# A four-layer graph network on one core: gathered edge rows for more target tiles and stages, tiles in another order

## The reference, cut to what matters

```python
h = relu(layernorm(x)); x = x + L0(h)   # hypergraph convolution, twice: m = segment_sum(xt[src], dst) / B
                                        #                                out = segment_sum(m[dst], src) / D
h = relu(layernorm(x)); x = x + L1(h)   # red = segment_sum(h[src] + relvectors[type], dst); GRU cell(red, h)
h = relu(layernorm(x)); x = x + L2(h)   # GCN: out = segment_sum(norm * (h @ W.T)[src], dst), self loops; layernorm; relu
h = relu(layernorm(x)); x = x + L3(h)   # attention: softmax over heads of the first n edges' two ends
```

## Time and profile before

| | us |
|---|---|
| three runs | 1287.16, 1292.99, 1293.87 (median 1292.99) |
| the profiled execution, its own time | 1292.79 |
| its span | 1289.8 |
| busy: PE, DVE, ACT, POOL | 1192.9 (92%), 701.2 (54%), 444.1 (34%), 269.8 (21%) |
| chain that ended last, by engine | PE 80%, DVE 7%, POOL 6%, DMA 2%, ACT 2%, issue 2% |

### The profile page before, as it was taken

One profiled execution on the slowest core, in us unless ns is written; L12 is line 12 of the kernel. 1 busy time (PEld: TensorE's weight loads), 2 busy tenths in 40 slices (PEclk: granted clock), 3 DMA queues, 4 the chain that ended last, 5 costly groups with the idle time before them and its releaser, 6 DMA issues.

```text
span 1289.8 us, 23482 instructions
## 1 busy us (share of the span) xinstructions
PE 1192.9 (92%) x9431; PEld 934.7 (72%) x9431; DVE 701.2 (54%) x1974; ACT 444.1 (34%) x948; POOL 269.8 (21%) x438
## 2 busy tenths in 40 slices
PE   2699999999999998989999999999999998999990
PEld 1456666768989995556888888676777767898970
DVE  7866456774555655545354552434435364655556
ACT  2745554428766651112112121221212222212123
POOL 6820000112000004566011110000100011355310
PEclk9989999999999999989999999999999999999995
DMA  4210000004122212322444331011101101122103
GB/s 169 73 32 1 1 2 1 1 1 162 64 69 77 76 64 81 104 77 83 127 145 167 133 113 59 25 38 32 43 25 38 37 30 55 34 59 61 36 9 101
DMA packets 48801, 80.77 MB, mean 63 GB/s; under 512 B 8617, under 2 KB 30597, under 8 KB 48688
## 3 DMA queue, kind: packets, MB, share of 16 engines
q1 hardware_dynamic: 37420, 54.52, 12.7%
q0 software_dynamic: 7136, 14.07, 3.9%
q10 hardware_dynamic: 4132, 10.63, 2.3%
HBM read 49.29 MB, written 29.89 MB: 61 GB/s over the span
## 4 chain that ended last, share of the span: by engine, by line
PE 80%; DVE 7%; POOL 6%; DMA 2%; issue 2%; ACT 2%; SPq 0%; DVEq 0%; ACTq 0%
PE ps L478 39%; PE ps L1992 11%; PE ps L817 5%; PE ps L2016 4%; PE ps L783 3%; PE ps L890 3%; PE ps L892 3%; PE ps L772 3%; PE ps L916 2%; POOL pairA L1699 2%; PE ps L896 2%; PE ps L894 2%; PE ps L862 1%; POOL whh L745 1%; POOL work L745 1%
## 5 line engine op out<-in xcount | busy, mean ns | idle before, releaser
L478 PE MATMUL ps<-big,pairB 125*128 125x250 fp8e4 (+1 forms) x2600 | 304.5, 268 | 0.6 <-DVE big L1255 0.6
L478 PEld LDWEIGHTS ps<-big,pairB 125*128 125x128 f16 x2600 | 239.6, 98 | 30.8 <-issue 2.8
L1992 PE MATMUL ps<-pairA,adj 125*125 125x512 f16 x625 | 208.1, 406 | 0.0
L727 POOL TENSOR_TENSOR st<-st,mhalf 125x1 f32<-125x1 f32 x100 | 62.0, 620 | 509.8 <-DVE st L1375 509.4
L478 PE MATMUL ps<-adj,pairB 125*128 125x250 fp8e4 (+1 forms) x1300 | 146.3, 267 | 1.8 <-DVE pairB L1433 1.8
L478 PE MATMUL ps<-adj,pairA 125*128 125x250 fp8e4 (+1 forms) x1300 | 139.2, 267 | 0.0
L478 PEld LDWEIGHTS ps<-adj,pairB 125*128 125x128 f16 x1300 | 123.3, 99 | 16.2 <-DVE pairB L1433 2.1
L478 PEld LDWEIGHTS ps<-adj,pairA 125*128 125x128 f16 x1300 | 120.9, 98 | 19.3 <-issue 7.7
L1929 ACT ACTIVATE adj<-ps 125x450 fp8e4<-125x450 f32 (+6 forms) x191 | 97.3, 518 | 103.5 <-PE ps L2018 103.0
L2018 PEld LDWEIGHTS ps<-wih 128*128 128x128 bf16 x615 | 84.6, 144 | 51.9 <-issue 1.3
L2018 PE MATMUL ps<-wih 128*128 128x7 bf16 (+5 forms) x615 | 101.9, 178 | 0.0
(11 more groups left out here) (316 smaller groups left out, 1841.8 us busy)
## 6 DMA issues: line engine op xcount, KB each, us to landing
t_adjTp<-big SPq DMA_DIRECT2D x25, 400.0 KB, 2.6
...
```

Of the source, the lines that this page charges most:

```text
L478: last = pe.matmul(out, src[:, j, FEAT * part + 128 * c:FEAT * part + 128 * (c + 1)], rhs(j, p), start=(n + part == 0 and not begun), stop ...
L727: g.tensor_tensor(st[:, 9:10], st[:, 8:9], k.mhalf[:, 0:1], ALU.pow).then_inc(S[rstd], 1)
L1992: last = pe.matmul(k.ps[0:P, 6 + t % 2, :], k.adj[:, j, PITCH * i:PITCH * i + P], k.pairA[:, j, :], start=(j == 0), stop=(j == TILES - 1))
```

## The change

1. Tiles 14 to 24 may be gathered. The lists of a tile are as many as its expected edges need (`LISTS`: 12, 11, 11, 11, 10, 10, 10, 10, 10, 9, 9 for tiles 14 to 24, 113 in all), not 10 for all.
2. In the build the first mean of tiles 17 to 24 (`BUILD_FAR`) is gathered: 79 lists instead of 8 x 25 dense matmuls. `ORDER` and the new `SUMS` (order of the means) differ, and `SUMMED` is spread evenly over the slots. The source rows are stored to `t_pairs` at the start of the build.
3. The second mean gathers tiles 18 to 24 as before (68 lists); its one-hots are all made in the first turns, in free columns of `adj`, and the ring has more buffers. `overlay` and `ballot` move to back1.
4. The GRU gathers tiles 14 to 24 (113 lists, four matmuls of 125 columns each), the GCN tiles 20 to 24 (48 lists, and four such matmuls for each tile's own row). Groups come in the order `GRU_GROUPS`, `GCN_GROUPS`. Each stage's input rows are stored to a table (two DMAs a tile) before its first gather.
5. POOL's list: gathers stand ahead of `deviation(i)` in the numbers of `GRU_PACE` and `GCN_PACE`; the z gathers stand behind by `BASE_PACE`.

By the tables 504 aggregate units stand in the build instead of 625 (`SUMMED` at slot 72: 35 instead of 75, at slot 136: 90 instead of 183), and 518 units in the second mean instead of 520.

```diff
-ORDER = tuple(range(TILES - 1, -1, -1))
+ORDER = (*range(16, 12, -1), *range(24, 19, -1), *range(12, 8, -1), 19, 18, *range(8, -1, -1), 17)
-SPARSE, EACH = 7, 10
-DENSE = TILES - SPARSE
-GATHERS = SPARSE * EACH
-AHEAD = 4
+FAR, BUILD_FAR, MEAN_FAR, GCN_FAR = 14, 17, 18, 20
+def list_length(tile):
+    share = math.sqrt((tile + 1) / TILES) - math.sqrt(tile / TILES)
+    mean = EDGES * share
+    return math.ceil((mean + 3.4 * math.sqrt(mean * (1 - share))) / SLOT)
+LISTS = [list_length(t) for t in range(FAR, TILES)]
+GATHERS = sum(LISTS)
+def list_of(tile):
+    at = sum(LISTS[:tile - FAR])
+    return range(at, at + LISTS[tile - FAR])
+FIRST_GATHER, GATHER_SLOTS = 168, 3.8
 def summing():
-    marks = [0, STOP[1] + 5] + [STOP[t] + 5 for t in range(2, TILES)]
-    share = [0, 0] + [TILES * (TILES - 1) * (t - 1) / (TILES - 2) for t in range(2, TILES)]
+    near, far = [i for i in ORDER if i < BUILD_FAR], list(range(TILES - 1, BUILD_FAR - 1, -1))
+    units = {i: TILES if i < BUILD_FAR else LISTS[i - FAR] for i in ORDER}
+    ready = {i: STOP[ORDER.index(i)] + 5 for i in near}
+    for n, i in enumerate(far):
+        ready[i] = max(STOP[ORDER.index(i)] + 30, FIRST_GATHER + 8 + GATHER_SLOTS * sum(units[t] for t in far[:n + 1]))
+    total, done, left, order, out = sum(units.values()), 0, 0, [], []
+    for s in range(SLOTS):
+        while done < total * (s - 32) / (SLOTS - 32):
+            if not left:
+                turn = next((x[0] for x in (far, near) if x and ready[x[0]] <= s and not (order and x is far and order[-1] >= BUILD_FAR)), None)
+                if turn is None:
+                    break
+                (far if turn >= BUILD_FAR else near).remove(turn)
+                order.append(turn)
+                left = units[turn]
+            left, done = left - 1, done + 1
+        out.append(done)
+    return order + near + far, units, out
-MEAN_GAPS = (4, 3, 2, 2, 3, 2, 2)
-MEAN_ORDER = [i for n, gap in enumerate(MEAN_GAPS)
-              for i in (*range(sum(MEAN_GAPS[:n]), sum(MEAN_GAPS[:n + 1])), DENSE + n)]
+MEAN_GAPS = (6, 2, 2, 2, 2, 2, 2)
+MEAN_ORDER = [i for n, gap in enumerate(MEAN_GAPS)
+              for i in (*range(sum(MEAN_GAPS[:n]), sum(MEAN_GAPS[:n + 1])), MEAN_FAR + n)]
+GRU_GROUPS = (0, 1, 2, 7, 3, 8, 4, 9, 5, 10, 6, 11, 12)
+GCN_GROUPS = (0, 1, 2, 3, 10, 4, 5, 11, 6, 7, 8, 9, 12)
+GRU_ORDER, GCN_ORDER = ([t for g in groups for t in range(2 * g, min(2 * g + 2, TILES))] for groups in (GRU_GROUPS, GCN_GROUPS))
+HOT_ORDER = [*range(MEAN_FAR, TILES), *range(FAR, MEAN_FAR)]
+def visiting():
     out = []
-    for s in range(SLOTS):
-        n = max(m for m, at in enumerate(marks) if at <= s)
-        part = (s - marks[n]) / (marks[n + 1] - marks[n]) if n + 1 < len(marks) else 0
-        upto = share[n] + part * (share[min(n + 1, TILES - 1)] - share[n])
-        out.append(min(TILES * sum(stop + 5 <= s for stop in STOP), round(upto)))
+    for stage, order, first in ((0, SUMS, BUILD_FAR), (1, MEAN_ORDER, MEAN_FAR), (2, GRU_ORDER, FAR), (3, GCN_ORDER, GCN_FAR)):
+        for turn, tile in enumerate(order):
+            if tile >= first:
+                start = out[-1].stop if out else 0
+                out.append(Visit(stage, tile, min(turn, 21) if stage == 3 else turn, start, start + LISTS[tile - FAR]))
+GRU_PACE = (22,) + (5,) * (TILES - 1)
+GCN_PACE = (14, 3, 3, 0, 0, 3, 3, 2, 2, 3, 3, 3, 0, 0, 0, 0, 0, 2, 3, 3, 1, 0, 0, 0, 0)
+BASE_PACE = (0, 0, 0, 3, 3, 0, 0, 1, 1, 0, 0, 0, 3, 3, 3, 3, 3, 2, 0, 0, 0, 0, 0, 0, 0)
...
+        def gather(q, n, s):
+            wait_past(pool, F["used"], max(HOME[n][1] + 1, VISITS[q - 3].stop if q >= 3 else 0))
+            g.indirect_dma_start(gathered(k, n), None, d["pairs2" if VISITS[q].stage == 3 else "pairs"], bass.IndirectOffsetOnAxis(ap=k.far_src[:, s:s + 1], axis=0)
+                                 ).then_inc(landed(k, q)[0], 16)
+        pool.wait_ge(k.paired, 2 * 32 * TILES)
+        for one in gathers(1):
+            gather(*one)
         for i in range(TILES):
             deviation(i, k.st[i % 2], B, "var", "rstd", "nmr")
+        pool.wait_ge(k.paired, 3 * 32 * TILES)
+        pool.wait_ge(indexed, 64)
+        waiting = gathers(2)
         for i in range(TILES):
-            deviation(i, k.st[i % 2], G, "var", "rstd", "nmr", k.dinvu)
+            for one in itertools.islice(waiting, GRU_PACE[i]):
+                gather(*one)
+            deviation(i, k.st[i % 2], G, "var", "rstd", "nmr", k.dinvu[:, GRU_ORDER[i]:GRU_ORDER[i] + 1])
+        pool.wait_ge(k.paired, 4 * 32 * TILES)
+        waiting = gathers(3)
         for i in range(TILES):
+            for one in itertools.islice(waiting, GCN_PACE[i]):
+                gather(*one)
             deviation(i, k.st[i % 2], C, "var", "rstd")
             deviation(i, k.st2[i % 2], C, "var2", "rstd2", "nmr2")
-            if i == 5:
+            if i == 3:
                 pool.wait_ge(T["hot"], 1)
                 pool.wait_ge(T["base"], 16)
-            if 5 <= i < 18:
-                for t in range(2 * (i - 5), min(2 * (i - 5) + 2, TILES)):
-                    g.indirect_dma_start(far_z(t), None, d["z0"][:, :], bass.IndirectOffsetOnAxis(ap=idx[:, 1, t:t + 1], axis=0)
-                                         ).then_inc(T["far"], 16)
+            for t in range(sum(BASE_PACE[:i]), sum(BASE_PACE[:i + 1])):
+                g.indirect_dma_start(far_z(t), None, d["z0"][:, :], bass.IndirectOffsetOnAxis(ap=idx[:, 1, t:t + 1], axis=0)
+                                     ).then_inc(T["far"], 16)
...
+        def far_sums(stage, p, groups, bank, half, a, b):
+            tile = 2 * groups[p] + half
+            q = VISIT[stage, tile]
+            if a == 0:
+                pe.wait_ge(*landed(k, q))
+                pe.wait_ge(*hot_known(tile))
+            for m in range(a, min(b, LISTS[tile - FAR])):
+                x, s = gathered(k, VISITS[q].start + m), list_of(tile)[m]
+                for c in range(KC):
+                    at = 2 * P * c if tile == TILES - 1 else 2 * P * c + P * half
+                    for part in range(2):
+                        last = pe.matmul(k.ps[0:128, bank, at:at + P], x[:, FEAT * part + 128 * c:FEAT * part + 128 * (c + 1)], hots[s],
+                                         start=False, stop=True, skip_group_check=True)
                 last.then_inc(F["used"], 1)
+            far, pair = GRU_GROUPS[p] >= FAR // 2, len(group_tiles(GRU_GROUPS[p])) == 2
+            if far and pair:
+                far_gru(p, 1)
+            elif far:
+                far_gru(p, 0, 4)
+            else:
+                if p >= 3:
+                    gru(p, 0, 0, EARLY)
+                gru(p, 0, EARLY, TILES)
             if p >= 1:
                 turn_hold(p)
-            gru(p, 1, 0, TILES)
+            if p + 1 < NP and GRU_GROUPS[p + 1] >= FAR // 2:
+                far_gru(p + 1, 0, 0, 128 if p + 2 < NP else 4)
+            if not far:
+                gru(p, 1, 0, TILES)
...
+            far = GCN_GROUPS[p] >= GCN_FAR // 2
+            ahead = p + 1 < NP and GCN_GROUPS[p + 1] >= GCN_FAR // 2
             for u in range(2 * TILES):
-                if p >= 3 or u >= EARLY:
+                if far:
+                    if u % 5 == 0 and p + 1 < NP:
+                        far_gcn(p, 1, u // 5, u // 5 + 1 if u < 45 else 128)
+                elif p >= 3 or u >= EARLY:
                     gcn(p, u // TILES, u % TILES, u % TILES + 1)
+                if ahead and u % 2 == 1:
+                    n = (u - TILES) // 2 if p + 2 < NP else (u - 9) // 2
+                    if 0 <= n < LISTS[2 * GCN_GROUPS[p + 1] - FAR]:
+                        far_gcn(p + 1, 0, n, n + 1)
...
+        visits = [(q, n, s) for q, visit in enumerate(VISITS) if visit.stage == 0
+                  for n, s in zip(range(visit.start, visit.stop), list_of(visit.tile))]
+        for t, i in enumerate(SUMS):
+            while visits and FIRST_GATHER + GATHER_SLOTS * visits[0][1] < END[t] + 20:
+                q, n, s = visits.pop(0)
+                if n == 0:
+                    pool.wait_ge(turned, ALL)
+                    g.memset(k.adj.rearrange("p j (t c) -> p j t c", c=PITCH)[:, :, :, P:PITCH], 0.0).then_inc(padded, 1)
+                    pool.wait_ge(k.paired, 32 * TILES)
+                    pool.wait_ge(h_out, 16 * BATCH)
+                    pool.wait_ge(iotas, 2)
+                    pool.wait_ge(indexed, 4)
+                wait_past(pool, F["used"], max(HOME[n][1] + 1, VISITS[q - 3].stop if q >= 3 else 0))
+                g.indirect_dma_start(gathered(k, n), None, d["pairs"], bass.IndirectOffsetOnAxis(ap=k.far_src[:, s:s + 1], axis=0)
+                                     ).then_inc(landed(k, q)[0], 16)
```

More of the change, by code:

```diff
@@ L11 @@
+import itertools
 import math
@@ new lines, in summing @@
+    return order + near + far, units, out
+STOP = [max(b.stop for b in BLOCKS if b.turn == t) for t in range(TILES)]
+SUMS, UNITS, SUMMED = summing()
+UPTO = [sum(UNITS[i] for i in SUMS[:n]) for n in range(TILES + 1)]
```

(50 more changed lines are left out.)

350 lines of the change are left out of this document (213 added, 137 removed).

## The result

The median went from 1291.41 us (four runs, 1287.16 to 1293.87) to 1347.7 (four runs, 1340.42 to 1353.33): ratio 1.043, 95% interval 1.0377 to 1.0483. 1279 was predicted, with a range up to 1308. The profiled execution took 1340.42 us.

What follows compares the result with a forecast made beforehand. The prediction took PE to bound the kernel, with 80% of the chain of waits. Its terms, build -13.5, back1 +1, second mean -17.5, GRU -20, GCN +36, sum to -14: from 1293 to 1279 us, range 1232 to 1308.

Steps and rivals of the forecast that it cites:

- the pitches: PE's time per matmul: 0.2158 us for 512 columns in the mean, 0.110 for 250 columns, 0.057 for 125.
- GCN, +36 forecast: GCN stage: POOL's queue sets the pace, 14 gathers delay the first deviation, PE's saving doesn't count; bounds -10 to +60.
- The wait for tile 24's list in the GRU: GRU: PE wants this list at about 1000 and it lands at 1010, behind the deviation of turn 18; +10.7 us.
- The keys in the build: Build before slot 72: DVE's keys set the date, so removing 40 aggregates only makes PE wait 8.6 us longer.
- gathers cost PE only where a list is late: All gathering stages: a gather takes 1.35 us of POOL; PE loses time only by waiting for its list.
- The second mean's miss of 12.2: Second mean: forecast -17.5 us, 496 units running without waits at gathered tiles if POOL keeps up; bounds 0 to -18.
- The build, -13.5 forecast: Build: 121 aggregates fewer are 26.1 us of PE, but only the 81 after slot 72 pay, less 4; bounds -26 to 0.
- the 4 us taken off for slot 136: Build: deduction from 17.5 us of saving, for aggregates leaving before slot 136 while DVE makes no one-hots.
- The GRU's lower bound: GRU: the -20 us term, PE alone -34.9, had bounds -35 and -10, the latter counting the losses twice.
- A: Rival: PE decides everywhere, gathers stay hidden at 1.24 us each; -76, 1217 us; chance 0.17.
- C: Rival: POOL's gathers are slower in GCN, build and GRU; at 1.8 us each 1318, middle 1305; chance 0.25.
- D: Rival: gathers starve in the build alone, where DVE is busiest, 2.07 us each; 1324 us; chance 0.05.

Runs made afterwards that it cites:

- e1: Changed kernel with another POOL order in the GCN: three gathers ahead of the first deviation instead of 14, some between a tile's two deviations; 1331.57 us, ratio 1.0343.
- e2: Kernel before plus 22 gathers that nobody reads, in one unbroken row at the start of the GRU; ratio 1.0179.
- e5: Kernel before plus 22 unread gathers at the start of the GRU, POOL waiting after every fourth until it has landed; ratio 1.0014.
- e8: Changed kernel with e1's GCN order and a wait for landing after every 8 gathers in the build, 10 in the mean, 6 in the GRU; ratio 1.0181.
- e15: e11 with the changed even spread (`SUMMED`) alone, tiles in the old order, no gathers in the build; 1291.74 us, ratio 0.9989.
- e16: e11 with the changed tile order (`ORDER`) alone, its spread kept; 1283.92 us, ratio 0.9922.
- e17: e11 with fewer lists: 68 in the GRU and 28 in the GCN, rows of at most four gathers in the GRU; 1332.91 us, ratio 1.0301.
- e11: e8 with the build of the kernel before: its tile order, its spread, no gathers there; 1281.23 us, ratio 0.9903.
- e13: e11 with 90 GRU lists in rows of four, plus the changed build order and spread without gathers in the build; ratio 1.0178.
- e6: Changed kernel with e1's GCN order, two POOL waits in the second mean, 8 + 8 gathers before the first GRU deviation; ratio 1.0403.
- e9: As e8 with shorter rows: 4 gathers in the build, 5 in the mean, 4 in the GRU and GCN; ratio 1.0452.
- e14: e13 with 28 lists (tiles 22 to 24) gathered in the build in rows of four; ratio 1.0123.
- e4: Kernel before plus 22 unread loads at the start of the GRU as plain DMAs on SP's queue instead of gathers; ratio 1.0001.

## Why the prediction was wrong

The prediction for the profiled run was 1289.8 - 14 = 1275.8 us of span; it was 1337.2, 61.4 more. Of these 24.9 are the build, 12.2 the mean, 23.1 the GRU, 3.0 the GCN.

**Where it holds.** The bound (PE, 80% of the chain) and the pitches. back1: +1.0 as forecast. GCN, +36 forecast, +39.0 measured, and by the mechanism named, as far as e1 can tell: 24.6 of them are the order of POOL's list. The first deviation was forecast 21 us after PE resumes, and POOL, after the row of 14 gathers, gets to it at

```profile
1089.58 1.01 POOL L867 DMA_INDIRECT b<-t_pairs,far_src  x1 [3.76 <-DMA t_pairs<-pairB]
...
1105.94 0.95 POOL L867 DMA_INDIRECT pairA<-t_pairs,far_src  x1 [0.31 <-issue]
1106.91 0.59 POOL L840 TENSOR_TENSOR st<-st,mhalf 125x1 f32<-125x1 f32 x1
```

19.5 us after 1087.4, where the GRU ended. The parts fit too: PE's transposes of the fourth tile come 13.6 us later than before, counted from the stage's start, for 15.1 forecast, and from there to tile 19 another 22.1 for 20. The wait for tile 24's list in the GRU was forecast at +10.7:

```profile
PE ps L981 <- DMA b<-t_pairs,far_src: 10.8, 1, 10.8
```

The keys in the build: forecast 8.6 us longer idle before slot 72, measured 21.2 for 13.9, +7.3; the wait ahead of it:

```profile
78.70 1.11 PE L2273 MATMUL ps<-ident,adj 128*128 128x128 f32 x4 [4.67 <-DVE adj L1997]
```

**The step that failed in three stages: gathers cost PE only where a list is late.** The prediction took 1.35 us of POOL for a gather and nothing of PE. The pitch was even 1.25. But in the GRU a dense row of them stops PE again and again after some 10 us, shown by e2 (22 in a row, +21.1 us of GRU in an otherwise unchanged kernel) against e5 (same gathers, pauses: 0). The GRU's miss of 23.1 us has the size of e2's, and PE's idle time without a releaser is 15.4 us in one and 15.6 in the other. Cutting the row in the changed kernel didn't bring the forecast 277.7 us: e8 takes 295.3 and e15 289.8, since loads and lists come late there. The second mean's miss of 12.2 goes when the rows are cut: e15, e16 and e17, which also place their gathered tiles a little differently, have a mean of 112.9 us with PE idle for 0.0, and 130.5 - 17.5 = 113.0 was the forecast. (In e11, 114.9, PE waits 1.9 us ahead of the last gathered tile, whose last gather starts only at 597.0; in e8, 121.2, the same rows of ten did stutter.) That term was right but for the row of 24.

Before, nothing in the rows spoke of this. The second mean of before even has a row of 20 gathers, from 532.8 to 560.2, with 0.30 us between any two. Its first and last, and all of PE's waits from 530 to 562:

```profile
532.78 0.94 POOL L745 DMA_INDIRECT W<-t_pairs,far_src  x1 [9.09 <-PE ps L831]
...
559.21 0.94 POOL L745 DMA_INDIRECT whh<-t_pairs,far_src  x1 [0.30 <-issue]
```
```profile
PE ps L831 <- DMA W<-t_pairs,far_src: 4.5, 1, 4.5
PE ps L831 <- DMA whh<-t_pairs,far_src: 0.6, 1, 0.6
```

PE waits only for lists. So a long row doesn't always make PE stutter. This one has 1.39 us from start to start where e2 and the changed GRU have 1.25, and PE runs matmuls of 512 columns there, one each 0.2158 us, where the GRU's follow each 0.110; the changed mean, with 1.31 us from start to start, stutters late, after 20 us. Which of the two decides, no run separates.

**The build, -13.5 forecast, +11.4 measured.** Two causes. First, order and spread: the prediction charged 8.6 + 4 = 12.6 us for the 93 aggregates that leave the time before slot 136; e13 measures 18.7 for its own spread and the order, of which e15 gives 12.9 to the spread and e16 5.4 to the tile order, for which the prediction had no term. In e15 the spread moves 71 aggregates past slot 136, at 0.18 us each; 93 at that price are an estimate of 17 us, so the 4 us taken off for slot 136 were too little by about 4. Second, the 79 gathers. By e13, 303.7 us of build, less 121 x 0.2158 = 26.1, would be 277.6; it is 298.6, 21.0 more (16 more if the 22 aggregates that leave before slot 136, where PE has idle time anyway, give nothing back; two other traces with this build code, e1 and e6, have 302.3 and 304.1). The trace shows stutter in the rows here too, late one-hots and gathers that are themselves longer than elsewhere (least, median, most ns):

```profile
L1935 POOL DMA_INDIRECT ho<-t_pairs,far_src x8: 945/973/4000, 129.6 to 238.7; - x8
```
```profile
L867 POOL DMA_INDIRECT big<-t_pairs,far_src x28: 941/949/1167, 801.3 to 1032.5; - x28
```

All 79 sum to 92.4 us, 1.17 each, and 1.47 with the issue. How this divides among the three is not settled: rows of 8 (e8, 308.7) and of 4 (e9, 321.9) made the build longer, not shorter, probably because the lists are then late. 28 gathers in rows of 4 (e14) cost 3.6 us beyond e13 less 9.7.

**Sizes of the forecast.** The GRU's lower bound, "-10 (the losses twice)", isn't its own sum: -34.9 + 2 x 14.9 is -5. The measured +3.1 lies outside either.

**The rivals.** A, PE decides everywhere, fell. C, gathers at 1.6 us or more, fell: 1.25 in GRU and GCN, though the time (1347.7) lies above its interval. D, starving in the build alone, has a part: some gathers of 2 to 4 us, but not the 2.07 for each. The Trainium skill (SBUF — State Buffer, section "Who interferes with whom") says that DVE holds up the descriptors of GpSimd gathers by a shared port. The long ones in the build, where DVE is busy 154 of 219 us, agree with that; the even 0.95 us of e2's row, with DVE idle, do too. The same section says that PE never waits on another engine. By that rule e2 would have cost nothing; it cost 21.1 us, and the measurement decides. Whether SBUF's ports have a part in it, no run shows.

What stops PE was not found. It is not the amount of bytes (e4), not DVE (e2's row), not PE's own instructions (e2's DMA view), not the sum of gathers (e5) and not the length of a row alone (the 20 of before). PE's starts fall on steps of about 0.70 us while it lasts; which resource that is, no run shows.
